# One Trainium2 core, conv-attention, attention-FFN and top-2 mixture in one kernel: routing weights sent through DRAM onto their experts' rows, relu and weight in one VectorE operation, third layernorm folded into keys, selector and weights

## The reference, cut to what matters

```python
t = t + _L1_attn_ref(_ln_t(t), ...)          # T1 in the kernel
t = t + _L1_ffn_ref(_ln_t(t), expert_sel, keys, values)

def _ln_t(v, eps=1e-05):
    m = jnp.mean(v, axis=-1, keepdims=True); s = jnp.var(v, axis=-1, keepdims=True)
    return (v - m) / jnp.sqrt(s + eps)

def _L1_ffn_ref(x, expert_sel, keys, values):       # E = H = 32, d = 128
    sel = jax.nn.sigmoid(xt @ expert_sel.T)
    sel_val, sel_idx = jax.lax.top_k(sel, 2)
    w = zeros((T, E)).at[arange(T)[:, None], sel_idx].add(sel_val)
    h = jax.nn.relu(jnp.einsum('td,edh->teh', xt, keys))
    out = jnp.einsum('teh,te,ehv->tv', h, w, values)
```

## Time and profile before

| what | before |
|---|---|
| time, median of 3 runs | 211.71 us (211.69 to 211.84) |
| the profiled execution's own time | 211.57 us |
| its span, first to last instruction | 209.8 us |
| PE busy | 196.0 us, 1625 instructions |
| DVE busy | 131.8 us |
| ACT busy | 131.7 us |
| POOL busy | 105.7 us |
| PE busy with fillers (L462) | 29.04 us |

### The profile page before, as it was taken

One profiled execution on the slowest core, in us unless ns is written; L12 is line 12 of the kernel. 1 busy time (PEld: TensorE's weight loads), 2 busy tenths in 40 slices (PEclk: granted clock), 3 DMA queues, 4 the chain that ended last, 5 costly groups with the idle time before them and its releaser, 6 DMA issues. The chain is left out here.

```text
span 209.8 us, 4691 instructions
## 1 busy us (share of the span) xinstructions
PE 196.0 (93%) x1625; PEld 141.8 (68%) x1638; DVE 131.8 (63%) x451; ACT 131.7 (63%) x256; POOL 105.7 (50%) x272
## 2 busy tenths in 40 slices
PE   7999899999989999999999999989998998999894
PEld 3655554557646877787879675867767877677683
DVE  1346776666878675986867777673663664464332
ACT  2344597988788697778689577756568427422220
POOL 4799795757475747714771534461452343311200
PEclk9999999999999999999999999999999999999999
DMA  6970000000000000000000000000000000000000
GB/s 173 354 256 0 6 0 0 5 0 3 0 0 3 2 3 0 27 3 0 5 2 25 3 0 3 25 0 3 27 0 5 0 25 2 3 25 0 30 0 25
DMA packets 6280, 5.46 MB, mean 26 GB/s; under 512 B 480, under 2 KB 5744, under 8 KB 6256
## 3 DMA queue, kind: packets, MB, share of 16 engines
q1 hardware_dynamic: 5952, 5.00, 7.5%
q10 hardware_dynamic: 304, 0.16, 0.2%
HBM read 4.10 MB, written 1.05 MB: 25 GB/s over the span
## 5 line engine op out<-in xcount | busy, mean ns | idle before, releaser
L748 ACT ACTIVATE EB_<-sc_ps 128x1024 f32<-128x1024 f32 x32 | 32.7, 1023 | 7.9 <-PE sc_ps L558 7.7
L657 PE MATMUL moe_ps<-val_sb,HWT 128*128 128x128 f32 x256 | 34.2, 276 | 0.7 <-DVE HWT L1057 0.7
L672 PE MATMUL hidden_ps<-XTT,keys_sb 128*128 128x256 f32 x128 | 34.3, 391 | 0.1
L1057 DVE TENSOR_TENSOR HWT<-hidden_ps,HR 128x512 f32<-128x512 f32 x32 | 22.0, 686 | 16.1 <-ACT HR L783 8.3
L657 PEld LDWEIGHTS moe_ps<-val_sb,HWT 128*128 128x128 f32 x256 | 31.0, 191 | 1.5 <-DVE HWT L1057 1.1
L783 ACT ACTIVATE HR<-hidden_ps 128x512 f32<-128x512 f32 x32 | 19.1, 597 | 14.9 <-PE hidden_ps L672 14.8
L672 PEld LDWEIGHTS hidden_ps<-XTT,keys_sb 128*128 128x128 f32 x128 | 22.0, 190 | 4.6 <-issue 2.1
L462 PE MATMUL hidden_ps<-idle_sb 128*128 128x512 bf16 x70 | 21.7, 417 | 1.8 <-DVE idle_sb L826 1.2
L558 PE MATMUL sc_ps<-HLT 32*128 32x256 f16 x256 | 19.5, 270 | 2.1 <-ACT EB_ L748 0.9
L1114 POOL TENSOR_SCALAR var<-mv 128x2 f32<-128x2 f32 x24 | 5.2, 218 | 26.7 <-DVE mv L835 25.9
L1116 POOL TENSOR_TENSOR rstd<-var,minushalf 128x2 f32<-128x2 f32 x24 | 16.8, 699 | 2.0
(11 more groups left out here) (179 smaller groups left out, 400.4 us busy)
## 6 DMA issues: line engine op xcount, KB each, us to landing
XT<-in_xT SPq DMA_DIRECT2D x8, 128.0 KB, 4.7
out<-OB SPq DMA_DIRECT2D x8, 128.0 KB, 1.8
X<-in_x SPq DMA_DIRECT2D x7, 128.0 KB, 4.7
keys_sb<-in_keys SPq DMA_DIRECT2D x1, 512.0 KB, 5.3
val_sb<-in_values SPq DMA_DIRECT2D x1, 512.0 KB, 6.3
pb_sb<-in_pb SPq DMA_DIRECT2D x1, 464.0 KB, 4.5
w2T_sb<-in_w2T SPq DMA_DIRECT2D x1, 256.0 KB, 4.3
pa_sb<-in_pa SPq DMA_DIRECT2D x1, 190.5 KB, 2.6
```

The lines of the kernel that those rows point to most:

```text
L657: last = mm(moe_ps[:, t * C:(t + 1) * C], HWT[:, k % 4, t * P:(t + 1) * P], val_sb[:, k, :], start=(k == 0 and t == 0), stop=(k == EB - 1) ...
L672: last = mm(hidden_ps[0][:, i * N:(i + 1) * N], keys_sb[:, k * EPB:(k + 1) * EPB, :].rearrange("p e h -> p (e h)"), XTT[:, b % 2, :], star ...
L748: fn(EB_[:, 2 * p:2 * p + 2, :, :].rearrange("p h t n -> p (h t n)"), both_ps[:, :], ACT.Exp, scale=1.0 / math.sqrt(DK)).then_inc(s_prob, 1)
L1057: V.tensor_tensor(HWT[:, half, :].rearrange("p i n -> p (i n)"), hidden_ps[1][:, :], HR[:, half, :].rearrange("p i n -> p (i n)"), ALU.mul ...
```

## The change

The weights are no longer spread by matmuls. VectorE makes the two-value copy and the weights W itself; TensorE turns W in fp32 into `hidden_ps[1]`; ScalarE copies it to WT (32 experts by 256 tokens); SP stores WT to a DRAM buffer (`moe_spread` on SP), waits for that store, and starts four DMAs that read it back, each repeating one expert's row over 32 partitions of WB (`moe_rows`). WB holds 8 KB on each of 128 partitions for one batch, 1 MB in all, twice. VectorE then does relu and weight in one `scalar_tensor_tensor` straight from `hidden_ps[0]`. ScalarE's relu and its tile HR are gone, and so are GpSimd's `moe_topk` and the building of `spread` in `prep_moe`.

The third layernorm is no longer applied to the tokens: T1 itself is turned. Keys and selector are centred once at the start by three matmuls with `cen` (identity less 1/128), and the scale by the reciprocal deviation goes into the exponential and into the sigmoid's denominator (`rinv`). T1 can be turned before its statistics are known; the exponential waits for them.

All four `ORDER` tables are rewritten and SP gets one. `warm_early` goes from 71 to 40 entries, `warm_late` from 33 to 9. TensorE's order at the end, after `ffn_output(7)`, is now moe_pair1(5), moe_spread(6), moe_pair2(5), moe_transpose(7), moe_pair3(5), moe_select(7), moe_output(5), moe_pair0(6), two fillers, moe_spread(7), moe_pair1 to 3(6), moe_output(6), moe_pair0(7), three fillers, moe_pair1 to 3(7), moe_output(7); before it was moe_spread(6), moe_pair0(6), seven fillers, moe_pair1(6), five fillers, moe_transpose(7), moe_pair2(6), moe_select(7), moe_pair3(6), a filler, moe_output(6), two fillers, moe_spread(7), moe_pair0(7), two fillers, moe_pair1 to 3(7), a filler, moe_output(7). On GpSimd `conv_scores` of batches 1 to 5 moves ahead of `proj_norm(0)`; before only batch 0's stood there.

```diff
         @block.sync
+            def moe_spread(b):
+                sp.wait_ge(s_wT, b + 1)
+                if b >= 2:
+                    sp.wait_ge(wb_in[b % 2], 16 * EPB * (b // 2))
+                sp.dma_start(w_dram[b % 2], WT[:, b % 2, :]).then_inc(w_out[b % 2], 16)
+            def moe_rows(b):
+                sp.wait_ge(w_out[b % 2], 16 * (b // 2 + 1))
+                if b >= 2:
+                    sp.wait_ge(s_hw, EB // 2 * (b - 1))
+                rows = w_dram[b % 2].rearrange("(k e) n -> e k n", e=EPB)
+                for e in range(EPB):
+                    sp.dma_start(WB[e * HE:(e + 1) * HE, b % 2], rows[e].partition_broadcast(HE)).then_inc(wb_in[b % 2], 16)
         @block.tensor
+            def prep_keys(i):
+                ...
+                mm(moe_ps[:, :], cen[:, :], keys_raw[:, i * 4 * P:(i + 1) * 4 * P], start=True, stop=True).then_inc(s_kc_ps, 1)
             def moe_transpose(b):
-                pe.wait_ge(s_xt, b + 1)
+                pe.wait_ge(s_t1, b + 1)
                 for t in range(TB):
-                    last = tr(ffn_ps[:, t * P:(t + 1) * P], XTK[:, b % 2, t, :], ident[:, :])
+                    last = tr(ffn_ps[:, t * P:(t + 1) * P], T1[:, b, t, :], ident[:, :])
             def moe_spread(b):
-                    last = tr(b16(moe_ps, F16)[0:3 * E, t * P:(t + 1) * P], WP[:, b, t].rearrange("p i e -> p (i e)"), identh[:, :])
+                    last = tr(hidden_ps[1][0:E, t * P:(t + 1) * P], W[:, b, t, :], ident[:, :])
             def moe_pair(b, q):
                 if n:
-                    pe.wait_ge(s_relu, n)
+                    pe.wait_ge(s_hw, n)
                 ...
-                for i in range(2):
-                    last = mm(hidden_ps[1][:, i * N:(i + 1) * N], spread[:, 2 * q + i, :], WT[:, b % 2, :], start=True, stop=True)
-                last.then_inc(s_moe_ps, 1)
         @block.scalar
             def moe_select(b):
                 act.wait_ge(s_sel_ps, b + 1)
-                fn(SE[:, b].rearrange("p t e -> p (t e)"), ffn_ps[:, 0:TB * E], ACT.Exp, scale=-1.0).then_inc(s_sel_e, 1)
+                act.wait_ge(s_u_rstd, b + 1)
+                for t in range(TB):
+                    last = fn(SE[:, b, t, :], ffn_ps[:, t * E:(t + 1) * E], ACT.Exp, scale=rstd[:, 3, b, t:t + 1])
-            def moe_pair(b, q):
-                fn(HR[:, ...].rearrange("p i n -> p (i n)"), hidden_ps[0][:, :], ACT.Relu).then_inc(s_relu, 1)
         @block.vector
             def norm_third(b):
                 norm_stats(b, T1[:, b], 3, s_u_stats, s_u_mv)
-                norm_apply(b, XTK[:, b % 2], T1[:, b], 3, s_u_rstd, s_xt)
             def moe_pair(b, q):
-                dve.wait_ge(s_moe_ps, n + 1)
-                dve.wait_ge(s_relu, n + 1)
+                dve.wait_ge(s_keys_ps, n + 1)
+                if q == 0:
+                    dve.wait_ge(wb_in[b % 2], 16 * EPB * (b // 2 + 1))
                 ...
-                V.tensor_tensor(HWT[...], hidden_ps[1][:, :], HR[...], ALU.mult).then_inc(s_hw, 1)
+                V.scalar_tensor_tensor(out=HWT[...], in0=hidden_ps[0][:, :], scalar=0.0, in1=WB[:, b % 2, 2 * q:2 * q + 2, :],
+                                       op0=ALU.max, op1=ALU.mult).then_inc(s_hw, 1)
         @block.gpsimd
             def prep_moe(b):
-                G.memset(spread[:, :, :], 0.0).then_inc(s_const_set, 1)
-                ...                                   # three affine_select of 32x1024
+                G.tensor_scalar(cen[:, :], ident[:, :], -1.0 / C, None, ALU.add).then_inc(s_cen, 1)
```

More of the change, by code:

```diff
@@ new lines @@
+        "conv_project": (0, 1, 21, 36, 53, 99, 125, 151),
+        "conv_stack": (5, 12, 31, 52, 75, 107, 136, 162),
+        "conv_scores": (8, 17, 35, 54, 79, 111, 141, 171),
+        "conv_turn": (15, 20, 41, 60, 92, 115, 144, 177),
+        "prep_sel": (16,),
+        "conv_output": (18, 22, 50, 73, 96, 118, 147, 180),
+        "prep_keys": (19, 56),
+        "attn_transpose": (37, 57, 82, 108, 129, 153, 173, 198),
[6 rows of a table added]
+        "attn_turn": (61, 74, 109, 126, 154, 179, 196, 221),
+        "attn_back": (65, 80, 114, 130, 159, 182, 202, 224),
@@ L87 @@
+        "moe_spread": (56, 78, 102, 121, 136, 147, 153, 156),
     },
     "vector": {
[L89 to L96, removed]
@@ L106 @@
[L106 to L110, removed]
[4 rows of a table removed]
-        "moe_output": (91, 119, 145, 160, 174, 186, 196, 201),
+        "conv_project": (0, 1, 10, 22, 30, 60, 85, 111),
+        "prep_phi": (2,),
+        "conv_stack": (3, 6, 17, 28, 42, 65, 92, 117),
@@ new lines @@
+        "conv_scores": (4, 7, 19, 31, 47, 67, 96, 123),
+        "conv_turn": (5, 11, 26, 39, 52, 70, 100, 133),
+        "conv_output": (8, 14, 27, 45, 58, 76, 102, 134),
+        "proj_norm": (9, 16, 29, 46, 64, 82, 104, 135),
+        "proj_angle": (12, 21, 34, 50, 69, 91, 110, 140),
+        "proj_reduce": (13, 24, 36, 54, 77, 94, 114, 141),
+        "proj_cos": (15, 25, 41, 59, 81, 103, 121, 143),
+        "proj_split": (18, 32, 44, 63, 84, 106, 122, 145),
+        "attn_transpose": (20, 33, 49, 66, 87, 108, 125, 148),
@@ L116 @@
+        "moe_topk": (62, 89, 118, 138, 158, 174, 182, 191),
[4 rows of a table added]
+        "moe_output": (95, 119, 147, 163, 179, 190, 196, 201),
     },
@@ L118 @@
         "prep_scan": (0,),
[L119 to L122, removed]
-        "proj_split": (8, 15, 22, 31, 40, 48, 56, 63),
-        "prep_w1": (9,),
-        "proj_angle": (12, 14, 17, 36, 41, 50, 64, 70),
-        "ffn_norm": (20, 27, 34, 47, 55, 61, 68, 74),
-        "ffn_cos": (21, 30, 39, 51, 59, 66, 73, 78),
-        "norm_second": (26, 37, 45, 57, 65, 71, 76, 80),
-        "norm_third": (28, 38, 46, 58, 67, 72, 77, 81),
-        "moe_topk": (33, 44, 54, 62, 69, 75, 79, 82),
+        "conv_scores": (1, 4, 5, 7, 8, 9, 17, 22),
+        "conv_project": (2, 3, 11, 14, 21, 33, 43, 50),
+        "prep_moe": (6,),
+        "proj_norm": (10, 13, 20, 27, 35, 42, 47, 57),
+        "proj_split": (12, 18, 25, 34, 40, 46, 51, 59),
+        "proj_angle": (15, 16, 26, 28, 36, 55, 61, 62),
+        "prep_w1": (19,),
+        "ffn_norm": (23, 30, 38, 45, 53, 58, 65, 69),
+        "ffn_cos": (24, 32, 41, 49, 56, 60, 66, 70),
+        "norm_second": (29, 37, 44, 52, 63, 67, 71, 73),
+        "norm_third": (31, 39, 48, 54, 64, 68, 72, 74),
+    },
+    "sync": {
+        "moe_spread": (0, 2, 4, 7, 11, 13, 17, 19),
+        "moe_rows": (1, 3, 5, 9, 12, 14, 18, 20),
+        "store": (6, 8, 10, 15, 16, 21, 22, 23),
     },
@@ L272, in build @@
         s_u_rstd = sem("s_u_rstd")
-        s_xt = sem("s_xt")
         s_xtT_ps = sem("s_xtT_ps")
@@ L301, in build @@
         moe_in = sem("moe_in")
+        val_in = sem("val_in")
+        w_out = [sem(f"w_out{i}") for i in range(2)]
+        wb_in = [sem(f"wb_in{i}") for i in range(2)]
+        w_dram = nc.dram_tensor("w_dram", [2, E, N], F32, kind="Internal").ap()
         ident = sb("ident", [P, P])
@@ L422, in build, with run_steps @@
         block = es.enter_context(nc.Block())
+        def run_steps(engine, steps):
+            for _, b, name in sorted((at, b, name) for name, row in ORDER[engine].items() for b, at in enumerate(row)):
+                step = name.rstrip("0123456789")
+                if name in steps:
+                    steps[name](b)
+                elif step in steps:
+                    steps[step](b, int(name[len(step):]))
         @block.sync
@@ L1048, in moe_topk @@
                 last.then_inc(s_rest, 1)
+                dve.wait_ge(s_rest, b + 1)
+                V.scalar_tensor_tensor(out=W[:, b], in0=SR[:, b, :, 0:E], scalar=0.0, in1=SG[:, b, :, 0:E],
+                                       op0=ALU.is_equal, op1=ALU.mult).then_inc(s_w, 1)
             def moe_pair(b, q):
```

225 lines of the change are left out of this document (108 added, 117 removed), and 43 rows, old and new, of the table ORDER.

## The result

| | before | after |
|---|---|---|
| device time, median (range) | 211.70 us (210.82 to 211.84) | 218.08 us (217.68 to 218.78) |
| ratio after / before, 95% interval | | 1.030 (1.028 to 1.032) |
| profiled execution, its span | 211.57, 209.8 us | 218.78, 217.0 us |
| PE busy, PE idle within the span | 196.0, 13.8 us | 188.4, 28.6 us |

The change makes the kernel 3% slower, where 201.9 us was forecast. The page of the kernel after: the engines' busy time (it answers to the earlier trace rows), the clock in 40 slices, and the shares of the chain of waits by engine.

A forecast was written before the change was run, and what follows sets the result against it. TensorE's queue was taken as the bound in the middle, chains of ACT, DVE and POOL at the start, PE, ACT and DVE at the end; -7.0 + 0.8 + 0.6 + 2.4 - 4.0 - 2.6 = -9.8, 201.9 us, range 194 to 209.

The forecast's parts named there:

- the way through DRAM: Weights' store and read back before each batch's first HWT: 7.1 us, exposing 0 to 1 us a batch, +2.4 us taken.
- the third rival: Read through DRAM at half rate: 10.2 us, DVE stands at each batch's first HWT; +15 us, 214.6 us; chance 0.10.
- The read: Four DMAs bringing the weights back from DRAM: 1.05 MB at 354 GB/s takes 3.0 us, with 1.4 fixed: 4.4 us.
- The store: Writing WT to DRAM: at most 1.8 us, from a 128 KB store's 1.8 us from issue to landing.
- Ahead of it: Transposes of W and the copy before the weights go to DRAM: 0.7 us.
- The cover: TensorE work between moe_spread and the batch's first HWT, to hide the round trip: 6.1 us batch 6, 7.3 batch 7.
- The fillers, early: 31 early fillers fewer, 6.6 us of PE's queue; batch 1's XR comes earlier; -4.0 us taken (0 to 6.6).
- HWT and the pair's cycle: Last pairs: HWT 0.72 us, cycle 1.85 instead of 1.99, some 8 pairs regain 0.14 each and not 0.22: +0.6 us.
- the second rival: Single PSUM tile: keys wait for DVE's HWT, 6.6 us return as PE idle, 208.5 us; chance 0.11.
- Spread matmuls, turn, centring, third layernorm, late fillers: Spread matmuls gone -7.0 us, fp32 turn of W +0.8, centring 0, third layernorm nothing counted, 24 late fillers fewer -2.6.
- The clock: PE's clock granted at half in a stretch such as 20 to 40 us: 214 us; chance 0.02.
- The signs named for a wrong forecast: DVE waiting several us for DMA, PE idle ahead of keys mid-kernel, clock row below 1.00, or early idle replacing fillers.

## Why the prediction was wrong

**The step that failed is the way through DRAM**, taken at +2.4 us. The kernel without it puts it at 15.7. That is the price of the third rival (+15, 214.6 us), by its mechanism: DVE stands at the first HWT, PE's keys behind it. The chance of 0.10 was far too small. The remaining 3.5 us up to the measured 218.1 are other terms, below. Three slips in the prediction's sums change nothing: the third rival comes to 214.5; its chance and the clock's add up to 0.12, where 0.11 stands for slower; 31 and 24 fillers at 0.215 us are 6.7 and 5.2 us, not 6.6 and 5.1. Part by part:

- *The read*, taken at 4.4 us, takes 7.5 to 8.2 us from first issue to HWT in seven batches (9.4 in the last, whose HWT also stands behind earlier pairs). The error is the rate: 354 GB/s was read from a slice whose transfers reach 128 partitions, and carried over to transfers onto 32, for which the trace had no row. These ran at 207 GB/s. The 177 GB/s worked out there from the Trainium skill's rule (SBUF — State Buffer, "Door 1: The DMA port swizzle") were nearer than the value taken. The four issues, 1.78 us, were not counted either.
- *The store*, taken at 1.8 at most with SP's handover inside the sum, takes 1.5 us to the first read in six batches and 2.0 and 2.9 in the other two; right in size.
- *Ahead of it*, 0.7 us were taken for turn and copy. From the start of the turn to the store's start are 0.8 to 1.1 us in five batches, but 1.4, 4.0 and 2.6 in batches 2, 3 and 4, where the copy of the weights stands in ScalarE's queue behind work of other batches. ScalarE's timeline ahead of the copy of batch 3, whose W was made at 127.91:

```profile
127.88 1.28 ACT L773 ACT_TABLE_LOAD   x1
130.53 0.42 ACT L773 ACTIVATE CS<-ARG 128x256 f32<-128x256 f32 x1 [1.36 <-DVE ARG L988]
130.85 0.57 ACT L793 COPY CT<-attn_ps 128x512 f32<-128x512 f32 x1
131.32 0.60 ACT L807 ACTIVATE HID<-ffn_ps 128x512 f32<-128x512 f32 x1
131.81 0.34 ACT L844 COPY WT<-hidden_ps 32x256 f32<-32x256 f32 x1
```

  The copy starts 3.9 us after W's start, for 0.34 us of work. The queue that a moved step stands in was asked for SP and DVE, and not for ScalarE.
- *The cover* was put too low, at 6.1 and 7.3 us in batches 6 and 7, where the kernel without the trip shows 8.3 and 8.4. The whole trip, counted from the turn, takes 9.8 to 13.6 us where 7.1 were taken, and goes past this too. So two errors of opposite sign met, and the one in the trip was the larger.

**The fillers, early**: right in its one named wait. T0 of batch 1 starts at 19.44 us, 19.5 was taken:

```profile
11.17 0.72 POOL L1178 TENSOR_TENSOR XR<-X,rc 128x256 f32<-128x256 f32 x1
19.44 0.60 DVE L945 SCALAR_TENSOR_TENSOR T<-hidden_ps,rden,XR 128x128 f32<-128x128 f32 x2
```

XR of batch 1 is started 9.5 us sooner and holds T0 no more. T1 of batch 1 starts at 70.31 us instead of 75.60, ahead of the first wait for DRAM: a lead of 5.3 us at this place, where 4.0 were taken for the stage. How much of it the early fillers gave was not tested; without the trip the lead is 2.1 us in batch 2 and 6.2 in batch 3. The trip then eats it: T1 of batch 3 is 3.3 us early, of batch 4 0.2 us, of batch 6 2.7 us late (119.51, 139.26, 170.89 before; 116.25, 139.03, 173.60 after).

**HWT and the pair's cycle**: HWT 0.687 us (0.72 taken), but the cycle is 1.91 us (1.85 taken), and the single tile costs 1.7 us where +0.6 stood in the sum. Right in kind, small in size. The argument against the second rival, that DVE's 15.2 us of waits ahead of HWT go, was wrong: without the trip DVE still waits 15.2 us there, now for the keys.

**Spread matmuls, turn, centring, third layernorm, late fillers** were not tried one by one. Together with the early fillers and the pair they were put at -12.2 us, 199.5 us without the trip; measured without it 202.4. Of the 2.9 us missing 1.1 are the single tile. Some 0.7 go with the clock: two executions without the trip ran at a mean clock of 0.998 and 0.999 and took 201.9 and 201.5 us, two at 0.982 and 0.983 took 202.9, and the median lies between. The rest stays open. What is missing shows in the drain: from T1 to OB of the last batch are 22.8 us without the trip, 20.3 before, and 21.6 with half the bytes, long runs and two tiles.

**The clock** was a rival by itself, for a stretch early in the kernel. It fell late, for the most part behind the waits for the rows, and with five fillers in those waits the time hardly moved.

The signs named for a wrong forecast (DVE waiting for the DMA, PE idle ahead of keys in the middle, a clock row below 1.00) are the ones that came.

## What to carry to other kernels

A tensor that goes through DRAM between two steps is priced by its whole trip: queue of the engine that copies, store, wait, issues, read, each from a row of its own; where no row has the read's shape (partitions reached, dimension outermost), the nearest rate is a bound and not an estimate. The work that is to cover the trip is better measured than summed: a kernel that leaves the dependence out shows it. The cheapest repair here was size: fp16 on the way turned +3% into -4%. A low clock behind a wait is to be tested by filling the wait before it is blamed.

## What the runs showed of the hardware that was not expected

- One transfer of 1.05 MB onto 128 partitions whose DRAM side has four rows outermost showed 2 to 3 tenths of the DMA engines busy, and the kernel took 311.8 us; four transfers onto 32 partitions each showed up to 9 tenths.
- Transfers onto 32 partitions ran at 207 to 223 GB/s for fp32 rows, with one row read 32 times or with 32 rows; onto 128 partitions at 313. With fp16 rows they ran at 227 in runs of 512 bytes and at 272 in runs of 4 KB.
- The output's store, on the same queue as the reads, lands 5.1 us after its issue instead of 1.8, 2.8 with half the bytes, and 2.1 with half the bytes in long runs.
